# A decoder layer on one core: layer norm scaling moved to POOL, its variance chain to ACT, patch distances straight from PSUM

## The reference

```python
x = layernorm(x + mamba(x))          # in_proj, conv of 4 taps, selective scan over 224 steps, out_proj
x = layernorm(x + depool(x, ctx))    # rmsnorm(x) @ W_in + a decaying sum over patches + x
x = layernorm(x + moe(x))            # 8 experts, top 1, capacity 448 rows each
# layernorm(x) = (x - mean) / sqrt(var + 1e-5)
# rmsnorm(x)   = x * rsqrt(mean(x * x) + 1e-5)
```

## Time and profile before

| what | value |
|---|---|
| median of three runs | 3315.78 us (3312.24 to 3319.89) |
| span of the profiled execution | 3316.6 us |
| busy in it: PE, DVE, ACT, POOL | 2744.6, 2714.3, 1798.4, 1625.1 us |
| a steady step of the first phase | 153.6 us, with DVE busy for 148.4 us |

### The profile page before, as it was taken

The page is one execution under the profiler, slowest core; times in us unless marked ns, Lnnn a source line. Parts: engine busy times, 40 slices in busy tenths (PEclk is TensorE's granted clock), DMA queues, the critical chain, the costliest instruction groups (busy, mean ns, idle before and its releaser), DMA issues.

```text
span 3316.6 us, 37616 instructions
## 1 busy us (share of the span) xinstructions
PE 2744.6 (83%) x11840; PEld 2204.1 (66%) x11840; DVE 2714.3 (82%) x2657; ACT 1798.4 (54%) x3846; POOL 1625.1 (49%) x868
## 2 busy tenths in 40 slices
PE   4677978888787878787888788887877799999998
PEld 4566665757566666566666657576655588888886
DVE  6999999999999998999899999999997344444442
ACT  3566757565656666566657575656563333333331
POOL 1766666666666666665666665766663000000000
PEclk8899999999998999999999999999988799999999
DMA  8120202020120102020202020210202233333330
GB/s 285 41 62 6 68 12 73 7 73 29 50 63 17 65 15 65 14 73 6 74 12 67 12 73 10 69 50 24 65 9 102 83 123 118 110 111 118 120 124 17
DMA packets 90362, 208.65 MB, mean 63 GB/s; under 512 B 7684, under 2 KB 16516, under 8 KB 89415
## 3 DMA queue, kind: packets, MB, share of 16 engines
q1 hardware_dynamic: 80934, 184.45, 16.9%
q0 software_dynamic: 5120, 14.21, 1.4%
q10 hardware_dynamic: 4096, 7.34, 0.7%
HBM read 176.53 MB, written 29.98 MB: 62 GB/s over the span
## 4 chain that ended last, share of the span: by engine, by line
DVE 27%; PE 26%; issue 26%; POOL 16%; ACT 2%; DMA 2%; POOLq 0%; DVEq 0%; SPq 0%; ACTq 0%
POOL arena L800 12%; DVE ring L1047 10%; PE ring L1333 10%; PE work L1333 9%; DVE ring_sb L1047 7%; DVE arena L904 2%; PE y L1319 2%; DVE arena L1049 2%; PE work L1151 2%; POOL arena L747 1%; DMA arena<-bc_rows 1%; POOL arena L749 1%; PE work L1291 1%; DVE arena L875 1%; POOL arena L744 1%
## 5 line engine op out<-in xcount | busy, mean ns | idle before, releaser
L800 POOL TENSOR_TENSOR arena<-arena 128x896 f32<-128x896 f32 x512 | 1163.2, 2278 | 852.5 <-PE y L1319 837.4
L1319 PE MATMUL y<-arena,cst_sb 128*128 128x224 f32 x4096 | 992.1, 390 | 416.6 <-DVE arena L1049 415.5
L1319 PEld LDWEIGHTS y<-arena,cst_sb 128*128 128x128 f32 x4096 | 818.3, 207 | 569.9 <-DVE arena L1049 518.8
L1047 DVE TENSOR_TENSOR_SCAN ring<-ring,arena 128x896 f32<-128x896 f32 x352 | 711.5, 2021 | 31.3 <-POOL arena L800 25.3
L676 ACT ACTIVATE ring<-arena,small 128x224 f32<-128x224 f32 x1408 | 544.9, 436 | 277.3 <-DVE arena L1049 266.6
L1151 PE MATMUL work<-arena 128*128 128x224 f32 x2048 | 461.8, 372 | 38.8 <-DVE arena L904 27.4
L1047 DVE TENSOR_TENSOR_SCAN ring_sb<-ring_sb,arena 128x896 f32<-128x896 f32 x160 | 422.7, 2642 | 47.7 <-ACT ring_sb L676 47.5
L1151 PEld LDWEIGHTS work<-arena 128*128 128x128 f32 x2048 | 406.2, 202 | 64.4 <-DVE arena L904 31.4
L1102 DVE SCALAR_TENSOR_TENSOR hidden_lo<-work,hidden_hi 128x448 fp32r<-128x448 f32 x128 | 80.0, 625 | 387.9 <-ACT hidden_hi L714 387.9
L1049 DVE TENSOR_TENSOR arena<-ring,arena 128x896 f32<-128x896 f32 x352 | 384.2, 1091 | 12.0
L813 POOL DMA_INDIRECT out<-res,ids x32 | 42.7, 1336 | 670.6 <-DVE mst L1087 645.7
(11 more groups left out here) (146 smaller groups left out, 3719.2 us busy)
## 6 DMA issues: line engine op xcount, KB each, us to landing
weights<-in_w SPq DMA_DIRECT2D x64, 1024.0 KB, 6.9
arena<-bc_rows SPq DMA_DIRECT2D x128, 448.0 KB, 4.4
arena<-in_ctx SPq DMA_DIRECT2D x16, 896.0 KB, 5.7
expert_rows<-x2e SPq DMA_DIRECT2D x1, 7224.0 KB, 27.1
xrow<-expert_rows SPq DMA_DIRECT2D x8, 903.0 KB, 10.6
arena<-in_xT SPq DMA_DIRECT2D x16, 448.0 KB, 3.5
arena<-in_x SPq DMA_DIRECT2D x16, 448.0 KB, 3.5
out<-arena ACTq DMA_DIRECT2D x32, 224.0 KB, 2.3
```

Source lines behind the costliest of these rows:

```text
L800: nc.gpsimd.tensor_tensor(u[:, s % 4], dx[:, k:k + 1, :].to_broadcast([P, QN, L]), bc[:, 0, q * QN:(q + 1) * QN, :], ALU.mult).then_inc(u_ ...
L1047: nc.vector.tensor_tensor_scan(h, h, u_flat[:, s % 4, :], 0.0, ALU.mult, ALU.add).then_inc(scan_done, 1)
L1319: last = nc.tensor.matmul(o, ident, u[:, s % 4, i, :], start=False, stop=(q == Q - 1 and i == QN - 1))
```

## The change

- `normalise` moves from DVE to POOL, at POOL's side numbers 3, 6, 10 and 14. DVE's one-column instruction L876 goes. In its place `rstd_of` on ACT ends with a third instruction, variance times 1/std, and `rinv_of` passes 1/std again as the scale of its Ln.
- A new semaphore `normed` counts POOL's four calls of a sequence; those who read or overwrite the rows wait for it (ACT, PE and DVE).
- The patch distances: L941 (PSUM to `plug`) and two L944 (`plug` to `decay`) become two instructions that read the matmul's PSUM bank each. L946 stays.
- Token numbers: a table in the constants instead of a tile that DVE raises by 224 (L990) in each step. The copy L988 stays and reads the table.

```diff
@@ -91,7 +91,8 @@
         iota_e8 = const(2 * E).rearrange("p (h e) -> p h e", h=2)
-        token0, s_iota = const(2), const(2)
+        token0, s_iota = const(2 * NB).rearrange("p (b h) -> p b h", b=NB), const(2)
+        s_after, s_floor = const(2), const(2)
         eps, neg_depool = const(1), const(1)
...
@@ -449,22 +448,25 @@
-                act.wait_ge(mv_step, e * 16 + (4 * k + 2))
+                act.wait_ge(mv_step, e * 8 + (2 * k + 2))
                 nc.scalar.activation(ln[:, k, 2:3], ln[:, k, 1:2], ACT.Ln, bias=eps[0:H]).then_inc(ln_step, 1)
-                act.wait_ge(ln_step, e * 16 + (4 * k + 1))
+                act.wait_ge(ln_step, e * 20 + (5 * k + 1))
                 nc.scalar.activation(ln[:, k, 3:4], ln[:, k, 2:3], ACT.Exp, scale=-0.5).then_inc(ln_step, 1)
+                act.wait_ge(ln_step, e * 20 + (5 * k + 2))
+                nc.scalar.activation(ln[:, k, 4:5], ln[:, k, 1:2], ACT.Copy, scale=ln[:, k, 3:4]).then_inc(ln_step, 1)
...
-                act.wait_ge(mv_step, e * 16 + (4 * k + 4))
-                nc.scalar.activation(ln[:, k, 5:6], ln[:, k, 4:5], ACT.Ln, bias=eps[0:H]).then_inc(ln_step, 1)
-                act.wait_ge(ln_step, e * 16 + (4 * k + 3))
+                act.wait_ge(ln_step, e * 20 + (5 * k + 3))
+                nc.scalar.activation(ln[:, k, 5:6], ln[:, k, 4:5], ACT.Ln, scale=ln[:, k, 3:4], bias=eps[0:H]).then_inc(ln_step, 1)
+                act.wait_ge(ln_step, e * 20 + (5 * k + 4))
                 nc.scalar.activation(ln[:, k, 6:7], ln[:, k, 5:6], ACT.Exp, scale=-0.5).then_inc(ln_step, 1)
-                act.wait_ge(ln_step, e * 16 + (4 * k + 4))
+                act.wait_ge(ln_step, e * 20 + (5 * k + 5))
...
                 rinv_of(e, 2 + h)
+                act.wait_ge(normed, e * 4 + (3 + h))
                 nc.scalar.activation(hx[0:H, h], x2e[:, h, 0:D], ACT.Copy, scale=ln[:, 2 + h, 6:7]).then_inc(out0_ready, 1)
...
@@ -503,6 +505,7 @@
                     need(act, out0_stored, e * 32)
+                act.wait_ge(normed, e * 4 + (1 + h))
                 nc.scalar.activation(hx[0:H, h], r[0:H, h], ACT.Copy, scale=ln[:, h, 6:7]).then_inc(hx_ready, 1)
...
@@ -751,16 +754,37 @@
+            def normalise(e, k, h, out):
+
+                pool.wait_ge(ln_step, e * 20 + (5 * k + 2))
+                apart(pool)
+                nc.gpsimd.tensor_scalar(out, r[0:H, h], ln[:, k, 0:1], ln[:, k, 3:4], ALU.subtract, ALU.mult).then_inc(normed, 1)
+
             def side(b, par):
...
                 nxt, e, e2 = b + 1, b - 1, b - 2
+                if tail:
+                    yield 3
+                    if isinstance(b, int) and b == 2:
+                        pool.wait_ge(s_prefill, 16)
+                    need(pool, scattered, e2 * 32)
+                    normalise(e2, 2, 0, x2e[:, 0, 0:D])
+                    yield 6
+                    normalise(e2, 3, 1, x2e[:, 1, 0:D])
                 if pro:
...
                     nc.gpsimd.tensor_tensor(xn, xT, rinv[:, 1:2, :].to_broadcast([P, DC, L]), ALU.mult).then_inc(xn_ready, 1)
+                if epi:
+                    yield 10
+                    normalise(e, 0, 0, r[0:H, 0])
                 if scan:
...
                     make_delta(b, 2, par)
+                if epi:
+                    yield 14
+                    normalise(e, 1, 1, r[0:H, 1])
+                if scan:
                     yield 15
...
@@ -863,21 +886,16 @@
                 job_copied(dve, step_of, name)
-                n = e * 16 + 4 * k
+                n = e * 8 + 2 * k
                 nc.vector.bn_stats(st[:], r[0:H, h]).then_inc(mv_step, 1)
...
-            def normalise(e, k, h, out):
-
-                dve.wait_ge(ln_step, e * 16 + (4 * k + 2))
-                nc.vector.tensor_scalar(out, r[0:H, h], ln[:, k, 0:1], ln[:, k, 3:4], ALU.subtract, ALU.mult).then_inc(mv_step, 1)
-                nc.vector.tensor_scalar(ln[:, k, 4:5], ln[:, k, 1:2], ln[:, k, 3:4], ln[:, k, 3:4], ALU.mult, ALU.mult).then_inc(mv_step, 1)
-
             def layer_norm2(step_of, e, h):
                 bank, free = job_full(dve, step_of, f"xatt{h}")
+                dve.wait_ge(normed, e * 4 + (1 + h))
                 nc.vector.tensor_tensor(r[0:H, h], r[0:H, h], bank[0:H, 0:D], ALU.add).then_inc(free, 1)
...
@@ -913,6 +931,7 @@
                 dve.wait_ge(x_res_loaded, e * 16 + 16)
+                need(dve, normed, e * 4 + (h - 1))
                 nc.vector.scalar_tensor_tensor(r[0:H, h], x_res[0:H, h], 2.0, bank[0:H, 0:D], ALU.mult, ALU.add).then_inc(free, 1)
...
@@ -930,24 +949,20 @@
                     need(dve, scattered, e2 * 32)
-                    normalise(e2, 2, 0, x2e[:, 0, 0:D])
                     layer_norm2(b - 1, e2, 1)
-                    yield 5
-                    normalise(e2, 3, 1, x2e[:, 1, 0:D])
                 if epi:
...
                     bank, free = job_full(dve, b, "plug")
-                    nc.vector.tensor_scalar(plug[:], bank[0:H, 0:L], -1.0, 0.0, ALU.add, ALU.max).then_inc(free, 1)
+                    nc.vector.tensor_scalar(decay[0:H, 0, :], bank[0:H, 0:L], s_after[0:H, 0:1], s_floor[0:H, 0:1],
+                                            ALU.subtract, ALU.max).then_inc(kk_step, 2)
+                    nc.vector.tensor_scalar(decay[0:H, 1, :], bank[0:H, 0:L], s_after[0:H, 1:2], s_floor[0:H, 1:2],
+                                            ALU.subtract, ALU.max).then_inc(free, 1)
+                    dve.wait_ge(kk_step, e * 4 + 3)
                     job_copied(dve, b, "plug")
-                    for c in range(2):
-                        nc.vector.tensor_scalar(decay[0:H, c, :], plug[:], s_iota[0:H, c:c + 1], None, ALU.subtract).then_inc(kk_step, 1)
-                    dve.wait_ge(kk_step, e * 4 + 3)
                     nc.vector.scalar_tensor_tensor(decay[0:H], decay[0:H], -1000.0, decay[0:H], ALU.mult, ALU.max).then_inc(kk_step, 1)
...
                     residual(b, e, 0)
-                    yield 8
-                    normalise(e, 0, 0, r[0:H, 0])
                 if scan:
...
@@ -956,8 +971,6 @@
                     residual(b, e, 1)
-                    yield 12
-                    normalise(e, 1, 1, r[0:H, 1])
                 if tail:
...
@@ -985,9 +998,7 @@
                     nc.vector.reciprocal(x2e[:, :, D], rt[:, 2, :]).then_inc(rt_step, 1)
-                    nc.vector.tensor_copy(x2e[:, :, D + 1], token[:]).then_inc(rt_step, 1)
-                    dve.wait_ge(rt_step, n + 9)
-                    nc.vector.tensor_scalar(token[:], token[:], float(L), None, ALU.add).then_inc(rt_step, 1)
+                    nc.vector.tensor_copy(x2e[:, :, D + 1], token0[0:H, bass.ds(e2, 1), :].rearrange("p o h -> p (o h)")).then_inc(rt_step, 2)
                 if pro:
...
@@ -1217,7 +1228,7 @@
                     if tail and slot == 8:
-                        pe.wait_ge(mv_step, e2 * 16 + (4 * 2 + 3))
+                        pe.wait_ge(normed, e2 * 4 + 3)
                         transposes(b, "tx0", x2e[:, 0])
...
@@ -1241,7 +1252,7 @@
                     yield 9
-                    pe.wait_ge(mv_step, e2 * 16 + (4 * 3 + 3))
+                    pe.wait_ge(normed, e2 * 4 + 4)
                     transposes(b, "tx1", x2e[:, 1])
...
@@ -1408,14 +1419,15 @@
-    cst = np.zeros((P, 2 * P + H + 2 * L + 4 * E + 6), np.float32)
+    cst = np.zeros((P, 2 * P + H + 2 * L + 4 * E + 2 * NB + 8), np.float32)
...
+    s_of = rows[:, None] + H * np.arange(2)[None, :]
+    tok_of = (s_of[:, None, :] + L * np.arange(NB)[None, :, None]).reshape(H, 2 * NB)
...
-                  rows[:, None] + H * np.arange(2)[None, :], rows[:, None] + H * np.arange(2)[None, :],
-                  np.full((P, 1), 1e-5), np.full((P, 1), -0.001)):
+                  tok_of, s_of, s_of + 1, -s_of, np.full((P, 1), 1e-5), np.full((P, 1), -0.001)):
...
```

More of the change, by code:

```diff
@@ L113, in build_decoder @@
         decay = sb("decay", [H + 1, 2, L])
-        plug = sb("plug", [H, L])
         mask = sb("mask", [H, 2, NB])
@@ L123, in build_decoder @@
         oh_sum = sb("oh_sum", [H, E])
-        token = sb("token", [H, 2])
         ring_sb = sb("ring_sb", [P, SUB])
@@ L229, in build_decoder @@
         kk_step, g_ready = map(sem, ("patch_distance_step", "depool_weights_ready"))
-        mv_step, ln_step, hx_ready, out0_ready, out0_stored = map(sem, (
-            "moments_step", "rstd_step", "hx_ready", "out0_ready", "out0_stored"))
+        mv_step, ln_step, normed, hx_ready, out0_ready, out0_stored = map(sem, (
+            "moments_step", "rstd_step", "rows_normalised", "hx_ready", "out0_ready", "out0_stored"))
         rt_step, ex_ready, scattered = map(sem, ("router_step", "router_exp_ready", "rows_scattered"))
@@ L852, in _ @@
                 nc.vector.tensor_scalar(diag[:, k, :], ident, d_skip[:, k:k + 1], None, ALU.mult).then_inc(s_weights, 1)
-            nc.vector.tensor_copy(token[:], token0[0:H]).then_inc(s_weights, 1)
             def patch_masks(batches):
@@ L1181, in cross @@
                 if isinstance(b, int) and b == 1:
```

(4 more changed lines are left out.)

## The result

The change makes the kernel slower. The median of four runs went from 3314.46 us (3312.24 to 3319.89) to 3363.55 us (3355.59 to 3364.94), a ratio of 1.0134 with a 95% interval of 1.0113 to 1.0156. The forecast was 3257.

What follows compares the result with a forecast made beforehand. DVE was taken to bound the steady steps, busy 148.4 of 153.6 us. Bare work 47 plus held time 37, minus POOL's calls 21 and the tail 4, gave 59 us saved: 3257 against 3315.8, range 3192 to 3300.

Steps and rivals of the forecast that it cites:

- Bare work, -47 us: On DVE: unheld time of removed norm calls (29 us), one-column instructions (12), patch distances (3) and token numbers (3) is saved.
- So the added ACT time lies beside DVE's work: 0: On ACT: the third instruction per chain, some 0.3 us 64 times, delays nothing, as slot 10's decays end 4.7 us early.
- ACT or POOL sets the pace in places: Rival, chance 0.15: ACT's 4.7 us run out or POOL's series comes late; 2 us a step lost, gain 29 us, 3286.
- Saved held time: 37 us: On DVE: of 97 us for which POOL held the removed instructions, 37 are saved; bounds 0 and 97.
- The rule of handing on: If a held DVE instruction goes, the next needing the same access waits for the same POOL instruction.
- side 8: DVE's norm call at side number 8, 2.33 us: L910 behind it takes over the hold, so nothing of 29 us is saved.
- POOL's calls, -21 us at 1.27 us each: 64 norm calls on POOL hold DVE for 13 us; shorter steps add 8; 14 or 33 lost with other call lengths.
- The price of 0.16 us per us: DVE is held 0.16 us per us of POOL work: 258 us on SBUF scans and multiplies against POOL's 1,625 busy.
- delays no u that DVE waits for: POOL, counted by slots, is ahead of DVE, so a 1.3 us call there makes no u late for DVE.
- The two engines share too much: Rival, chance 0.13: each POOL call microsecond is taken from DVE and all held time handed on; -38 us, 3354.
- threshold of 0.7 us a call: The cost to DVE of one POOL call, 47 / 64, from which that rival decides against the change.
- Tail, -4 us: Behind the last scan, five uncovered norm calls on the chain are each longer on POOL by 1.27 - 0.54 us; 4 lost.

Runs made afterwards that it cites:

- corr_late: The changed kernel with the softplus correction on DVE moved from behind slot 8 to behind slot 9 and its gating; 3335.26 us, 1.0046 of the kernel before.
- no_norm_01: The kernel before with the first layer norm's two scalings left out, its rows staying unscaled; 3297.84 us, 0.9934 of the kernel before.
- norm_on_dve: The changed kernel with its four norm calls back on DVE at the old side numbers, other parts kept; 3291.42 us, 0.9921 of the kernel before.
- norm_on_act: norm_on_dve_late with the four norm calls on ACT instead of DVE, plus two one-column instructions for the bias; 3285.16 us, 0.9908 of the kernel before.
- norm_on_dve_late: norm_on_dve with the softplus correction moved behind slot 9 and its gating; 3273.05 us, 0.9852 of the kernel before.
- no_norm_01_late: no_norm_01 with the softplus correction moved behind slot 9 and its gating; 3293.36 us, 0.9932 of the kernel before.
- before_late: The kernel before with only the softplus correction moved behind slot 9 and its gating; 3318.35 us, 1.0002 of the kernel before.
- the memset run: norm_on_dve with four POOL memsets of 112x256 added at each of the change's four places; 3340.73 us, 1.0072 of the kernel before.
- pool_extra_x2: norm_on_dve with two unused POOL subtract-and-scale instructions of 112x256 added at each of the change's four places; 3382.25 us, 1.0207 of the kernel before.

## Why the prediction was wrong

**Bare work, -47 us: right.** The rest fell by 42.3. The patch distances' 3 us did not come: the two new instructions take 0.51 and 0.50 us, not L941's 0.38, and from the first to L963 it is 1.04 us in the step shown (2137.46 to 2138.50), where it was 1.03. The rest of the shortfall is small and not taken apart.

**"So the added ACT time lies beside DVE's work: 0": this step failed first, and is the largest by the tally.** It compared one pair, ACT's decays of slot 10 with DVE's scan of slot 10, with 4.7 us between them. L910, 4.6 us earlier, waits for ACT's last softplus term, and there the slack was 1.5 us; L910's row stood in the same timeline. It also counted 2.4 us taken from DVE in that stretch where 8.1 went, since it left out the held time of the removed calls (which at this place did go) and that the patch distances move to an earlier slot. The term was 0 and measured +77 us of waiting. What it is worth at the end is less: corr_late takes the wait away and gets 29 us back, as more than half of the idle time saved turns into held time. In the text this stood as a rival ("ACT or POOL sets the pace in places"), at 2 us a step and a gain of 29 us left; it came at 5 us.

**Held time, "Saved held time: 37 us": the second failure.** The forecast for held time as a whole was 37 us saved and 21 added, 16 less; it came out 1 more, 413.4 before and 414.5 after. The runs without new POOL work show the first of the two: in no_norm_01 12 us were saved of some 37 removed, in norm_on_dve 12 of 26 (patch distances and tokens), and in norm_on_act, against norm_on_dve_late, nothing of 65. The rule of handing on was the right one, and at the place where it was worked out (side 8) no_norm_01 shows it. But I let it end with the next instruction of the list. Where that one read PSUM I booked the hold as saved, while the SBUF scans and L963 are held for longer now. Without new POOL work the held time stays at 390 to 417 us whether DVE has 64 calls, 32 or none (no_norm_01_late and before_late, counted as in the second table, have 382 and 399). A likely reason, argued and not shown: POOL waits for PE's sums, and these for DVE's multiplies, so POOL's instructions move along with DVE's and meet it again.

**POOL's calls, -21 us at 1.27 us each: the call mis-sized, and the shift of POOL's list put at nothing.** A call took 2.07 to 2.11 us, close to the upper bound of 2.4 and not to the two-input row that I took. The price of 0.16 us per us was meant for the direct hold, and for that it was about right: 16 us under the calls in the kernel after and 31 in corr_late, 0.12 and 0.23 us per us of their 134. What failed is that the step stops at "delays no u that DVE waits for". This came true: DVE is idle in front of its PSUM scans for 30.3 us, where it was 31.3. But a call also moves u and the rest of POOL's list against DVE's, and these then hold it elsewhere, for 22 us more in corr_late than in norm_on_act. All together a microsecond of added POOL work cost 0.35 to 0.7 us in the four comparisons above; 134 us by 0.35 is 47 us, where 21 were booked. That is the rival "The two engines share too much", whose threshold of 0.7 us a call was just reached. The prediction gave it 0.13. Its mechanism, a direct exchange of time, is only part of what happened. The Trainium skill's sentence (Perfetto Trace Analysis, Optimizing Scalar/DVE Operations) that moving work from DVE to GpSimd might not help because of the shared port agrees with the outcome: norm_on_dve to after is 0.9921 to 1.0134. Of these 71 us some 29 went with the wait for ACT.

**Tail, -4 us: not tested by itself.** The time outside the steady steps grew by 1.4 us in all.

In sum, by the tally: 42 us of bare work gained, 0 of held time, 85 lost to idle time; the phase is 44 us longer. The first failure alone, worth 29 us at the end, would have left a gain of 59 - 29 = 30. Held time and POOL's price turned the sign: with the wait taken away the change is still 0.5% slower (corr_late). The terms do not add up exactly, since idle and held time turn into each other.

**What stays open.** Why POOL's own instructions hold DVE for longer when something is put between them: the table shows under which of them the time stands, and the memset run that 50 us can come in this way with next to no direct hold, but no run moves POOL's list without adding to it, and the wait for 1/std in front of each dummy was not tried alone. Which part of the 46 to 70 us would come back with other side numbers on POOL was not measured. That the late correction gains 23 us in norm_on_dve (8 to 38 by the two intervals) and nothing in the kernel before, where DVE's list is longer by some 16 us, fits the slack of 1.5 us but was not taken apart further.

## What to carry to other kernels

Before taking work from the busiest engine, list every wait of that engine on others in the stretch, with its slack, not only the one that looks next: removed work was the cover of the tightest of them. Time for which instructions are held by another engine belongs to the pair of engines, not to the instruction; count it as saved only if the other engine's work goes. And work put on the engine that holds costs more than the time for which it holds by itself, since it moves everything behind it: add a dummy of that size and measure it.

## What the runs showed of the hardware

- A POOL subtract-and-scale of 112x512 with two per-partition scalars takes 2.07 us, as long as a two-input one of 128x896 (2.09 us); one of 112x256 took 1.57 us on average.
- A 16-column DVE instruction with two SBUF inputs was held for 2.9 us beyond its 0.17, through two POOL instructions in a row (2.08 and 1.12 us). DVE did not get in between them. A DVE instruction of 112x448 was held for 4.9 us beyond its 0.63 through three, and a copy of two columns took 4.37 us on average in pool_extra_x2, where the shortest of its form takes 0.15.
- 83.5 us of POOL memsets, which read nothing, held DVE for 3 us and made the kernel 50 us slower.
- Over 99% of the time for which DVE instructions took longer than the shortest of their form stands under a POOL instruction, in the kernel before (406 us) and after (413).
